# Splitting the first context chunk and regrouping the opening's transfers of a gated cross-attention kernel

## What is computed

```python
def xattn(query, ctx, pos, mask):                 # 32 heads, 8 key heads, 128 wide
    q = (query @ Wq); k = (ctx @ Wk); v = (ctx @ Wv)
    q, k = rope(q, pos), rope(k, pos)             # tables indexed by the positions
    a = softmax(where(mask == 0, -1e9, q @ k.T / sqrt(128)))
    return (a @ v) @ Wo
x = x + tanh(g_xattn) * xattn(layernorm(x), ctx, pos, mask)
x = x + tanh(g_ffn) * moe(layernorm(x))           # 3 experts, top 2, chosen by a router
```

## Time and profile before

| what | value |
|---|---|
| median of 3 runs | 702.85 us (702.29 to 703.09) |
| the profiled execution's own time | 702.05 us |
| its span | 700.3 us |
| granted TensorE clock, mean | 0.997 |
| PE busy | 691.8 us, 99% of the span |
| PE weight loads | 580.2 us |
| VectorE, ScalarE, GpSimd busy | 559.9, 361.4, 402.7 us |
| DMA | 70.84 MB, mean 101 GB/s |

### The profile page before, as it was taken

The page is one execution under the profiler, slowest core; times in us unless marked ns, Lnnn a source line. Parts: engine busy times, 40 slices in busy tenths (PEclk is TensorE's granted clock), DMA queues, the critical chain, the costliest instruction groups (busy, mean ns, idle before and its releaser), DMA issues.

```text
span 700.3 us, 11567 instructions
## 1 busy us (share of the span) xinstructions
PE 691.8 (99%) x3479; PEld 580.2 (83%) x3479; DVE 559.9 (80%) x951; ACT 361.4 (52%) x961; POOL 402.7 (57%) x345
## 2 busy tenths in 40 slices
PE   9999999999999999999999999999999999999998
PEld 7888887888888888888888888888888887688886
DVE  5788786887887887887887887887887997687785
ACT  5525624545545545545555555555555687653521
POOL 5788855666666666666666566666566655330000
PEclk9999999999999999999999999999999999999999
DMA  8997564321231221221221221222222422120001
GB/s 264 345 307 287 196 205 141 107 89 61 63 91 61 62 90 60 64 86 60 66 84 62 67 83 60 68 82 60 72 80 61 136 90 76 60 77 31 1 31 60
DMA packets 65071, 70.84 MB, mean 101 GB/s; under 512 B 7680, under 2 KB 41472, under 8 KB 65024
## 3 DMA queue, kind: packets, MB, share of 16 engines
q1 hardware_dynamic: 64496, 68.98, 30.6%
q0 software_dynamic: 384, 1.05, 0.5%
q10 hardware_dynamic: 144, 0.26, 0.1%
HBM read 51.40 MB, written 18.87 MB: 100 GB/s over the span
## 4 chain that ended last, share of the span: by engine, by line
PE 89%; DVE 4%; ACT 2%; POOL 1%; issue 1%; SPq 1%; DMA 1%; DVEq 0%; ACTq 0%; POOLq 0%
PE q L298 29%; PE y L288 28%; PE q L288 6%; PE o L665 6%; PE s L647 5%; PE pt L509 4%; PE s L649 2%; PE o L288 2%; PE pt L288 2%; PE s L288 1%; PE s L509 1%; PE y L531 1%; PE s L531 1%; ACT prob L980 1%; DVE split L1279 1%
## 5 line engine op out<-in xcount | busy, mean ns | idle before, releaser
L288 PE MATMUL y<-big,split 128*128 128x512 f32 (+1 forms) x864 | 209.4, 391 | 0.7 <-DVE split L1279 0.5
L288 PEld LDWEIGHTS y<-big,split 128*128 128x128 f32 x864 | 161.0, 188 | 34.6 <-DVE split L1279 1.6
L298 PE MATMUL q<-xT_hi,big 128*128 128x512 f32 x512 | 175.1, 403 | 0.0
L1217 POOL TENSOR_TENSOR roped<-rot 128x512 f32<-128x512 f32 x58 | 75.1, 1294 | 101.7 <-DVE rot L1305 101.7
L966 ACT ACTIVATE big<-roped 128x512 fp32r<-128x512 f32 x63 | 40.0, 635 | 141.6 <-POOL roped L1217 136.4
L298 PEld LDWEIGHTS q<-xT_hi,big 128*128 128x128 f32 x512 | 96.1, 188 | 19.2
L980 ACT ACTIVATE prob<-scores,nmax 128x128 f32<-128x128 f32 x256 | 99.8, 391 | 20.4 <-DVE nmax L1437 20.3
L1231 POOL TENSOR_TENSOR prob<-prob,prec 128x512 f32<-128x512 f32 x64 | 66.7, 1042 | 60.5 <-DVE prec L1442 60.5
L298 PE MATMUL q<-xT_lo,big 128*128 128x512 f32 x256 | 99.5, 389 | 0.0
L1220 POOL TENSOR_TENSOR big<-roped,big 128x512 fp32r<-128x512 f32 x63 | 81.7, 1297 | 13.2 <-ACT big L966 13.2
L1209 POOL TENSOR_TENSOR big<-wraw,big 128x512 fp32r<-128x512 f32 x64 | 83.1, 1298 | 0.0
(11 more groups left out here) (200 smaller groups left out, 1279.5 us busy)
## 6 DMA issues: line engine op xcount, KB each, us to landing
wraw<-in_L_xattn_Wq SPq DMA_DIRECT2D x32, 256.0 KB, 2.9
wraw<-in_L_xattn_Wo SPq DMA_DIRECT2D x32, 256.0 KB, 2.8
kv<-k_scratch SPq DMA_DIRECT2D x64, 128.0 KB, 2.5
kv<-v_scratch SPq DMA_DIRECT2D x64, 128.0 KB, 2.7
v_scratch<-split SPq DMA_DIRECT2D x12, 512.0 KB, 3.9
wraw<-in_L_ffn_w SPq DMA_DIRECT2D x24, 256.0 KB, 2.8
k_scratch<-split SPq DMA_DIRECT2D x10, 512.0 KB, 3.4
k_scratch<-kv SPq DMA_DIRECT2D x6, 512.0 KB, 3.5
```

Source lines behind the costliest of these rows:

```text
L288: mm = pe.matmul(bank_[:, :], stationary(s, c), moving(m, c), start=(c == 0 and n == 0), stop=(c == EC - 1 and n == 2))
L298: mm = pe.matmul(bank_[:, :].rearrange("p (b t) -> p b t", b=BH), weights[s][:, c, h * P:(h + 1) * P], source[m][:, half * BH:(half + 1) * ...
L1217: pool.tensor_tensor(roped[:, :], rot[:, 0, :], rot[:, 1, :], ALU.add).then_inc(q_roped, 1)
```

## The change

- The zero matmuls are seven, not nine.
- Context chunk 0 comes in two transfers, batches 0 and 1 (semaphore `c0_in`) and batches 2 and 3 (`c_in[0]`), 128 KB each, and ScalarE copies it in two halves (`c0_half`, then `c_hi`).
- ScalarE's queue issues Wv's chunks 0 to 3; SP issues context 0 to 3, and then the positions.
- VectorE copies all 512 columns of Wv 0; ScalarE's copy of half of them is gone.
- TensorE starts on batches 0 and 1 with the first half of the context chunk, and waits for the second half before batches 2 and 3.

```diff
-BLANKS = 9
+BLANKS = 7
...
+        c0_in, c0_half = sem("c0_in"), sem("c0_half")
...
-        w_hi, w_lo, w0_half = sem("w_hi"), sem("w_lo"), sem("w0_half")
+        w_hi, w_lo = sem("w_hi"), sem("w_lo")
...
-            for k in range(EC):
+            sp.dma_start(rows[:, 0, 0:2 * P], ctx_in[0, 0][:, 0:2 * P]).then_inc(c0_in, 16)
+            sp.dma_start(rows[:, 0, 2 * P:4 * P], ctx_in[0, 0][:, 2 * P:4 * P]).then_inc(c_in[0], 16)
+            for k in range(1, EC):
                 c_load(k)
-                if k >= 1:
-                    w_load(k, w_chunks[k]).then_inc(w_in[k % NW], 16)
-                else:
-                    sp.dma_start(posi[:, :], pos).then_inc(pos_in, 16)
+            sp.dma_start(posi[:, :], pos).then_inc(pos_in, 16)
             for n in range(EC, W_DVE):
                 c_load(n)
...
                 for c in range(EC - 1):
-                    pe.wait_ge(c_hi, c + 1)
                     pe.wait_ge(w_hi, c + 1)
                     if c == 0:
-                        pe.wait_ge(w0_half, 1)
-                    for b in range(BH):
+                        pe.wait_ge(c0_half, 1)
+                        part(c, 0, 0, 0)
+                        part(c, 1, 0, 0)
+                    pe.wait_ge(c_hi, c + 1)
+                    for b in range(2 if c == 0 else 0, BH):
                         part(c, b, 0, 0)
...
-            act.dma_start(wraw[:, 0, :], w_chunks[0]).then_inc(w_in[0], 16)
-            c_hi_(0)
-            act.wait_ge(w_in[0], 16)
-            act.activation(w_target(0)[0][0][:, 0, 0:256], wraw[:, 0, 0:256], ACT.Copy).then_inc(w0_half, 1)
+            for n in range(EC):
+                act.dma_start(wraw[:, n, :], w_chunks[n]).then_inc(w_in[n], 16)
+            act.wait_ge(c0_in, 16)
+            act.activation(piece(0, 0)[:, 0:2, :], staged(0)[:, 0:2, :], ACT.Copy).then_inc(c0_half, 1)
+            act.wait_ge(c_in[0], 16)
+            act.activation(piece(0, 0)[:, 2:4, :], staged(0)[:, 2:4, :], ACT.Copy).then_inc(c_hi, 1)
             act.wait_ge(w_hi, 1)
...
             dve.wait_ge(w_in[0], 16)
-            dve.tensor_copy(w_target(0)[0][0][:, 0, 256:512], wraw[:, 0, 256:512]).then_inc(w_hi, 1)
+            dve.tensor_copy(w_target(0)[0][0][:, 0, :], wraw[:, 0, :]).then_inc(w_hi, 1)
+            dve.wait_ge(c0_in, 16)
+            dve.wait_ge(c0_half, 1)
             c_lo_(0)
-            dve.wait_ge(w0_half, 1)
             w_lo_(0)
             dve.wait_ge(pos_in, 16)
```

## The result

The changed kernel takes 705.61 us (median of 5, 703.84 to 706.65) where the kernel before takes 702.67 (median of 5, 702.29 to 703.09): a ratio of 1.0041 with an interval of 1.0028 to 1.0054, so 2.9 us slower. The forecast was 705.0.

A forecast was written before the change was run, and what follows sets the result against it. PE was taken to bound the kernel, so opening losses reach the end: 0.89 us behind after the first stall, 1.25 more at the second, 2.14 on the 702.85 median gives 705.0 us, range 702.5 to 706.4.

The forecast's parts named there:

- What bounds: Whole kernel: PE busy 691.8 of 700.3 us, so a microsecond lost in the opening reaches the end almost whole.
- Earlier start: Opening: first real matmul at 5.2 us, 0.35 earlier, at the low clock worth 0.18 us (0 to 0.3).
- the rivals' last point: Opening: no earlier start, from Wv chunk 0 sharing or ScalarE's table load; worth 0.2 us at most, hidden by the stalls.
- Positions: SyncE's queue: the positions, now sixth, land at 9.2 us (8.3 to 9.8), with VectorE waiting for them.
- First stall: Seventeenth matmul: low part of chunk 1 starts at 10.02, PE goes on at 10.85; stall 1.07 us, net 0.89 behind.
- Second stall: Fifth value tile: context chunk 7 issued at 13.37, tile starts at 19.35; another 1.25 us, 2.14 behind in all.
- What is late next: Rope transposes: fourth gather 0 to 0.3 us late, taken as 0; Wk's chunks 4 to 7 costed at nothing.
- the 2.14: Sum: PE 2.14 us behind after both stalls, added to the 702.85 median to give 705.0.
- Positions in time: Rival, SyncE's queue: positions land by 8.1 us, no stall, 702.65 us; chance 0.13.
- Two queues faster: Rival, opening transfers: positions at 8.3, chunk 7 in 3.3 us, 0.7 behind, 703.55 us; chance 0.20.
- Late clock: Rival, chunk 0's matmuls: clock rises later, 1.6 us, nothing beside the forecast; in its place, or something unseen, 0.05.

The follow-up runs named there:

- a4: The kernel before with ScalarE's queue issuing all four Wv chunks, SyncE's queue context 0, the positions, then context 1 to 3: 703.79 us, ratio 1.0023.
- b3: The kernel before with one added wait: VectorE, behind the positions' steps, also waits until Wv chunk 3 has landed: 704.8 us, ratio 1.0031.
- d1: The kernel before with positions fourth on SyncE's queue, seven zero matmuls, VectorE's whole Wv 0 copy, two rope copies ahead of Wk chunks 8 and 9: 702.8 us.
- a2: The kernel before with only the positions' transfer moved, behind Wv chunk 3 on SyncE's queue: 704.89 us, ratio 1.0042.
- c2: The changed kernel itself, unedited, timed and profiled a second time against the kernel before: 706.0 us, ratio 1.004.
- b4: The changed kernel with ScalarE's first two rope copies moved ahead of its copies of Wk chunks 8 and 9: 704.66 us, ratio 1.003.
- c3: The kernel before with the positions' transfer fourth on SyncE's queue, behind context and Wv chunk 1: 701.66 us, ratio 0.9984.
- a1: The changed kernel with the positions' transfer third on SyncE's queue again, behind the two halves of context chunk 0: 704.09 us, ratio 1.0028.
- b2: The changed kernel with Wv chunks 1 to 3 back on SyncE's queue and the positions right behind chunk 0's halves; split kept: 703.92 us, ratio 1.0016.
- b1: The kernel before with seven zero matmuls and VectorE copying all 512 columns of Wv chunk 0, no transfer touched: 702.91 us, ratio 1.0007.
- c1: The kernel before with seven zero matmuls, VectorE's whole Wv 0 copy, and two rope copies ahead of Wk chunks 8 and 9: 702.85 us, ratio 1.0001.
- a3: The changed kernel with VectorE waiting for the positions only behind the low parts of context and Wv chunk 3: 708.73 us, ratio 1.0102.

## Why the prediction was right, point by point

- **What bounds.** Right in the main: no later wait took up what PE lost in the opening (3.06 us at the second key tile, 3.39 at the router's stretch, 2.9 in the median). The 0.3 between the first two is the wait for GpSimd near 90 to 120 us, which the prediction did not look at; it is 0.6 and 1.4 in the two profiles of the changed kernel, 0.2 before. Whether the change lengthens it was not tested; a4, b3 and d1 have 0.6 too.
- **Earlier start.** Forecast 5.2, worth 0.18. It started at 4.57 and 4.65: VectorE's cast could begin at 4.05 and 4.17, and it took the 0.43 worked out for it. Wv chunk 0 was there earlier in each of the six profiles with all of Wv on ScalarE's queue (cast from 4.05 to 4.41) than in the eight with it on SyncE's (4.50 to 4.86). The second half was mis-sized: I had its copy end by 5.4, it ended at 5.93, and PE waited 0.36. What was left of the gain vanished in the stalls, as the rivals' last point had it, though not by the delay of Wv chunk 0 that it named.
- **Positions.** Forecast to land at 9.2 (8.3 to 9.8): issued at 3.17, they took 6.4 us and landed at 9.6. By the Trainium skill ("DMA: Bandwidth & Descriptors", section "Queues, rings and completion order") the engines take turns between queues by packet. With it the half-width packets would lose bytes; the prediction set that aside for equal bytes. The trace sides with the rule. From 2.5 to 3.5 us of the changed kernel (queue; packets, MB, share of 16 engines):

```profile
q10 hardware_dynamic: 126, 0.23, 67.4%
q1 hardware_dynamic: 142, 0.13, 38.7%
...
posi<-in_pos_BxS SPq DMA_DIRECT2D x1, 4.0 KB, 6.4
```

  ScalarE's queue (q10) moved 0.23 MB with fewer packets than SyncE's (q1) needed for 0.13, where it had been 0.19 and 0.17. The figure that the prediction drew from the rule, 9.7, was the nearer one, by a few tenths. The lateness as such does not need it: in a2, with all chunks at full width and all but Wv chunk 0 on SyncE's queue, the positions landed at 9.3.
- **First stall.** Forecast: low part of chunk 1 at 10.02, PE on at 10.85, stall 1.07. Measured 10.28, 11.02, 1.17 (1.15 in c2). Shown by a2 (the move alone, a wait of 0.54) and b3 (the hold alone, 0.61).
- **Second stall.** Chunk 7's issue was forecast at 13.37 and came at 13.39, with some luck: the low part of chunk 1 was 0.26 late against the forecast, and VectorE, whose operands now all lay ready, reached the end of chunk 3's in 3.08 us where it had taken 3.32. The spare of 0.4 us that the prediction gives this chain in the kernel before leaves out the 0.14 that its own sum adds (16.82 + 0.14 against 17.21); it is 0.25. Chunk 7's flight of 3.87 was 3.1 in one profile and 4.4 in the other, so the fifth value tile came at 18.62 and at 19.98, forecast 19.35.
- **What is late next.** Here the prediction's step failed in size. "I cost them at nothing; what covers them is the two transposes and the first key tile's early chunks": the cover was looked for at PE's first use of Wk's chunks 4 to 7, and not in ScalarE's queue, where the copies of Wk's chunks 8 and 9 stand ahead of the rope copies that PE needs for its second pair of transposes. Those chunks are issued when the low part of chunk 4 frees its buffer, so they came late as well. These copies had little to spare: in the kernel before the second of them ends at 23.59, and the transposes that need it start at 24.02. The wait was 1.01 us in the first profile; b4 took it away. The gathers, costed at 0 with 0.3 as the bound, took 0.35 there (3.08 from the fifth value tile to the transposes, 2.73 before). In the second profile neither shows: there the positions' 0.3 and chunk 7's flight, half a microsecond longer than the mean I took, make up the same. So the 2.14 fell short of 3.0 by whichever of several nearly equal chains ended last, and a sum along one chain, at its mean, is a lower estimate. The mechanism was the forecast's; its size was 0.8 us short and inside the range.
- **Rivals.** Positions in time: fell. Two queues faster: fell. From 4.6 to 9.7 us both kernels moved the same, 331 GB/s before and 329 after, and the second queue alone costs (a4, 1.0023); there Wv chunk 1 passes context chunk 1, but whether that is the whole cost is open. Late clock: not in the two profiles of the changed kernel, seen in d1. The prediction never asked whether the positions' second place was itself a cost; a2, c3 and d1 show that it went with a later landing of context chunk 1, and c3's median hints at a price.
- **The parts do not add.** The late positions alone cost what the whole change costs (1.0042 and 1.0041). Yet the change without them still costs (a1, 1.0028), and so do the second queue alone (a4, 1.0023) and the split with the old queue order (b2, 1.0016). So the late positions are enough for the whole loss, and undoing them is not enough to be rid of it; how the delays cover one another was not measured.

## What to carry to other kernels

A small transfer that several engines wait for is cheap only by its bytes: its place in the queue decides when everything behind the wait, in the waiting engine's own row, can go on. Place it so that it lands ahead of its first use, but not ahead of large transfers that are needed sooner; here fourth place was at least as good as second, and last place cost 0.4%. When a wait moves an engine's queue, follow every chain that hangs on it, through other engines' program order too, since several chains with nearly equal slack end last in turn and an improvement of one alone shows nothing. A second queue did not add bandwidth here (331 and 329 GB/s); it changed who was served first. And before a median is read to a tenth of a per cent, the executions should be sorted by their granted clock: two sorts of execution of one kernel lay 2 us apart here, and a different share of each can look like a gain.

## What the runs showed of the hardware that I had not expected

- The 4 KB of positions, 128 pieces of 32 B, second on the queue: context chunk 1's copy starts at 6.49, 6.56, 6.27 and 6.79 (the kernel before, b1, c1, b3). With the positions behind it: 5.52, 5.18 and 5.28 (a2, c3, d1). The means are 1.2 us apart and its issue is only 0.46 earlier, so it took some 0.7 us longer on the way (an estimate from these starts) with the positions ahead of it. From 4.0 to 6.5 us the four moved 0.62 to 0.69 MB and the three 0.78 to 0.88, all on SyncE's queue. Whether that is due to the small pieces is open: in c3 and d1 they fly within the same stretch and do not slow it, and 4 KB in larger pieces were not tried. The waits list no time that TensorE lost to it.
- Two hardware queues shared by packets and not by bytes: 0.23 MB against 0.13 MB in one microsecond, above.
- The same 256 KB transfer at the same place of the same program took 3.1 us in one execution and 4.4 in another, while the rope gathers flew. In b3 it took 5.1. The medians of one kernel still agree to some 0.5 us (702.48 to 703.0 for the kernel before on four chips, 705.61 and 706.0 for the changed one), and single profiles differ in which chain ends last.
- Executions of one kernel come in two sorts, 2 us apart, which their mean granted clock tells apart. Of the fourteen profiles the seven with 0.999 or more show no fall. The other seven do, five of them in the router's stretch, behind sixteen matmuls of 4 columns, and a3 and b3 in the opening, behind their long waits. Why one execution has the fall in the router's stretch and another does not is open.
